# Message stage: segment sums of two groups in one pass of four column strips, gathers held once a piece

## The reference

```
xs = concat(x[src, :8], x[dst, :8]);  xv = concat(x[src, 8:], x[dst, 8:])   # 16 scalars, 16 vectors
h  = sqrt(2) * relu(emb @ W1 / sqrt(10));  w = (h @ W2 / 4).reshape(E, 7, 16, 8)
s, g  = scalar and gate sums over u of xs, (xv . y1), each times w      # 8 and 8 of an edge
v     = vector sums over u of xs * y1, xv, W3J(xv, y2), each times w    # 8 x 3 of an edge
msg   = concat(G * tanh(s), (G * tanh(g))[:, None] * v) * weight[:, None]
out   = segment_sum(msg, dst)
```

## Time and profile before

| | us |
|---|---|
| median of 3 runs | 5658.57 |
| lowest and highest | 5657.39, 5661.72 |
| profiled execution, device time | 5663.47 |
| its span | 5661.7 |
| loop of the first message stage | some 740 to 3230 |

### The profile page before, as it was taken

The page is one execution under the profiler, slowest core; times in us unless marked ns, Lnnn a source line. Parts: engine busy times, 40 slices in busy tenths (PEclk is TensorE's granted clock), DMA queues, the critical chain, the costliest instruction groups (busy, mean ns, idle before and its releaser), DMA issues. The chain is left out here.

```text
span 5661.7 us, 70210 instructions
## 1 busy us (share of the span) xinstructions
PE 4006.7 (71%) x20839; PEld 2129.7 (38%) x20839; DVE 3192.8 (56%) x5351; ACT 1475.9 (26%) x2862; POOL 3379.2 (60%) x3371
## 2 busy tenths in 40 slices
PE   0005888787888888877877860099898998999870
PEld 0002322222222222232222320077666666766650
DVE  4504776776767776677776763044444444455442
ACT  2002444444444444444444430000000000001000
POOL 5675555555555555555555417666666666666756
PEclk9999888888888888888888985599999989999985
DMA  8411111111111111111111101022222222222211
GB/s 300 114 38 18 38 37 36 37 37 37 37 35 33 36 37 31 34 37 37 37 37 37 35 18 22 18 41 45 43 43 43 42 43 43 43 42 48 46 27 24
DMA packets 266652, 252.42 MB, mean 45 GB/s; under 512 B 182208, under 2 KB 236936, under 8 KB 263777
## 3 DMA queue, kind: packets, MB, share of 16 engines
q1 hardware_dynamic: 157028, 174.83, 11.2%
q0 software_dynamic: 109024, 72.30, 9.0%
q10 hardware_dynamic: 462, 4.00, 0.2%
HBM read 160.54 MB, written 90.34 MB: 44 GB/s over the span
## 5 line engine op out<-in xcount | busy, mean ns | idle before, releaser
L612 POOL DMA_INDIRECT edge<-xp_d,idx x1440 | 1421.4, 987 | 1089.0 <-issue 419.4
L864 DVE TENSOR_TENSOR prod<-G_ps,hid 128x1000 f32<-128x1000 f32 x1200 | 1399.4, 1194 | 884.6 <-remote 410.6
L1198 POOL DMA_INDIRECT gxb<-tab_d,idxb x1200 | 1259.1, 1049 | 577.0 <-issue 334.4
L753 PE MATMUL G_ps<-FT,wst 32*128 32x500 f32 x4800 | 999.3, 685 | 362.7 <-DVE prod L864 244.4
L1233 PE MATMUL G_ps<-tb,hot 125*126 125x500 f32 (+1 forms) x3200 | 727.8, 378 | 395.5 <-DVE hotk L1255 301.1
L782 PE MATMUL R_ps<-prod,red 128*32 128x500 f32 x4800 | 923.8, 706 | 0.8 <-ACT rt L678 0.8
L1233 PEld LDWEIGHTS G_ps<-tb,hot 125*126 125x126 f32 x3200 | 572.0, 201 | 537.5 <-issue 446.8
L753 PEld LDWEIGHTS G_ps<-FT,wst 32*128 32x128 f32 x4800 | 270.7, 200 | 827.5 <-DVE prod L864 412.3
L773 PE MATMUL T_ps<-FT,wst 32*128 32x500 f32 x800 | 522.4, 737 | 3.1 <-issue 3.1
L666 ACT ACTIVATE FT<-T_ps 128x500 f32<-128x500 f32 x400 | 235.0, 588 | 856.3 <-PE G_ps L753 629.9
L782 PEld LDWEIGHTS R_ps<-prod,red 128*32 128x32 f32 x4800 | 180.8, 124 | 691.2 <-issue 445.5
(11 more groups left out here) (242 smaller groups left out, 4541.3 us busy)
## 6 DMA issues: line engine op xcount, KB each, us to landing
xd_d<-zeros SPq DMA_DIRECT2D x16, 1562.5 KB
y_d<-zrb SPq DMA_DIRECT2D x40, 595.0 KB
edge<-xp_d,idx POOLq DMA_INDIRECT x1440
xv<-xd_d SPq DMA_DIRECT2D x40, 560.0 KB
y_d<-zr SPq DMA_DIRECT2D x40, 560.0 KB
edge<-sel_d SPq DMA_DIRECT2D x40, 546.9 KB
gxb<-tab_d,idxb POOLq DMA_INDIRECT x1200
em<-in_edge_attr SPq DMA_DIRECT2D x40, 175.0 KB
```

What stands on the lines that cost most here:

```text
L612: nc.gpsimd.indirect_dma_start(out=edge_c[:, i, 8:8 + DIM], out_offset=None, in_=xp_d, in_offset=bass.IndirectOffsetOnAxis(col, 0)).then_i ...
L753: return Tn.matmul(G_ps[pair][:, a * 512:a * 512 + GW], wst[rows, r * 128:(r + 1) * 128], FT[k][rows, :], start=True, stop=True)
L864: V.tensor_tensor(prod[k][i][:, :].rearrange("p (a e) -> p a e", a=2), gv, hid[k][:, :].rearrange("p (a e) -> p a e", a=1).broadcast_to([1 ...
L1198: nc.gpsimd.indirect_dma_start(out=gx[h][:, c * T1:(c + 1) * T1], out_offset=None, in_=tab_d, in_offset=bass.IndirectOffsetOnAxis(idx[h][: ...
```

## The change

`red` gets a third block. `prod` gets four buffers a kind of product in place of two, so that both groups of a piece stand in it. The sums of a piece are made together, twelve matmuls in three rounds of four column strips (two strips a group), at three places: `sum_round` 0 behind round1 of the next even group, 1 at that group's end, 2 behind round1 of the odd group. One ScalarE copy (`rt`, 128 x 500) and four back transposes of 128 columns follow, where there were two copies and eight transposes. `Y_ps` is laid out in 64 columns an edge column. ScalarE's `high` and VectorE's `turned` and `along` run one piece further ahead, and the tail of a piece runs a group later. Waits that others cover are left out on ScalarE, VectorE and TensorE, and the semaphore `b_G` is split in `b_G` and `b_G2`. GpSimd's `pace` keeps the hold at column 0 alone, and the indices are copied eight at a time.

```
-                        if c == 2 and (not isinstance(p, int) or p > 2):
-                            hold(S("b_gs"), p * 2 - 4)
-                        if c == 5 and some(p):
-                            hold(S("b_mul"), p * 6 - 4)
...
-                                if c == 0 and s % PC == 0 and not fixed:
-                                    for q in range(s, s + PC):
-                                        hold(S(f"b_gx{q}"), t * 16 * PW + 16 * PW)
-                                    nc.gpsimd.tensor_copy(idx[:, i:i + C], src_i[:, bass.ds((p + RING) * PW, C)]).then_inc(S("b_ix"), 1)
-                                    hold(S("b_ix"), t * 2 + s // PC - 1)
+                                if c == 0 and not fixed:
+                                    nc.gpsimd.tensor_copy(idx[:, i:i + PW], src_i[:, bass.ds((p + RING) * PW, PW)]).then_inc(S("b_ix"), 1)
+                                    hold(S("b_ix"), p - RING + 1)
...
-                            if k == 1 and not (last and g + 3 >= G2):
-                                s = (g + 3) // 2
+                            if k == 0 and not (first and g < 4):
+                                tanh(t * RING + g // 2 - 2)
+                            if k == 0 and not (last and g + 4 >= G2):
+                                s = (g + 4) // 2
                                 high(t * RING + s, s % RING, t * 2 + s // PC)
+                            if k == 1 and not (first and g < 2):
+                                out_of_R(t * RING + g // 2 - 1)
...
-                        for a in range(2):
-                            for o in range(3):
-                                i = (o, (0, 2, 1)[o])[a]
-                                last = Tn.matmul(R_ps[32 * o:32 * o + 32, 0:GW], red[:, a * KF:(a + 1) * KF], prod[k][i][:, a * GW:(a + 1) * GW], start=(a == 0), stop=(a == 1))
+                    def sum_round(m, b, u):
+                        if u == 0:
+                            pe.wait_ge(S("b_mul"), m * 6 + 6)
+                            if some(m):
+                                pe.wait_ge(S("b_rt"), m)
+                        for q in range(4):
+                            pair, a = ((0, 0), (1, 0), (2, 0), (0, 1), (2, 1), (1, 1))[q % 2 * 3 + u]
+                            last = Tn.matmul(R_ps[32 * q:32 * q + 32, 0:GW], red[:, u * KF:(u + 1) * KF],
+                                             prod[b * 2 + q // 2][pair][:, a * GW:(a + 1) * GW], start=(u == 0), stop=(u == 2))
...
                             round1(n, k)
+                            if sums_due:
+                                sum_round(m, b, 2 * k)
                             if not (last and g >= G2 - 2):
                                 transposes(n + 2, g2, p2)
-                            if not (first and g < 2):
-                                back(n - 2, k)
                             round2(n, k)
                             if not (last and g == G2 - 1):
                                 hidden(n + 1, 1 - k)
-                            if not (first and g == 0):
-                                reduce(n - 1, 1 - k)
+                            if sums_due and k == 0:
+                                sum_round(m, b, 1)
+                            if sums_due and k == 1:
+                                back(m)
```

More of the change, by code:

```diff
@@ L249, in _ @@
                     nc.gpsimd.memset(edge_c[:, :, SD + 40:EW], 0.0)
-                    for i in range(2):
+                    for i in range(3):
                         blk = red[:, i * KF + i * MO:i * KF + (i + 1) * MO]
@@ L497, in gnn_resnorm_kernel @@
             hid = [sbt(f"hid{k}", [128, GW]) for k in range(2)]
-            prod = [[sbt(f"prod{k}_{i}", [128, 2 * GW]) for i in range(3)] for k in range(2)]
-            rt = [sbt(f"rt{k}", [96, GW]) for k in range(2)]
+            prod = [[sbt(f"prod{k}_{i}", [128, 2 * GW]) for i in range(3)] for k in range(4)]
+            rt = sbt("rt", [128, GW])
+            YW = 2 * KF
             O = two("O", C1 * DIM)
@@ L648, in gather_sums @@
                         act.wait_ge(S(f"b_z{h}"), t * NPC + i + 1)
-                        if some(ch):
+                        if i == 0 and some(ch):
                             act.wait_ge(S("b_st"), ch * 32)
@@ L816, in _ @@
                     turn(PAIRS - 1, last=True)
-                    reduce(NG - 1, 1)
-                    back(NG - 2, 0)
-                    back(NG - 1, 1)
+                    for u in range(3):
+                        sum_round(NPIECES - 1, 1, u)
+                    back(NPIECES - 1)
                 @block.vector
@@ L911, in turn @@
                             ch = t * 2 + h
+                            b = g % 4
                             scan = None
@@ L914, in turn @@
                                 scan = lambda: fill(gc, ch + 1, 1 - h)
-                            if 4 <= gc < 8 and not (first and h == 0):
-                                scan = lambda: sums(gc - 4, ch - 1, 1 - h)
-                            multiply(n, k, 0)
-                            multiply(n, k, 1)
-                            if k == 0 and not (first and g < 4):
-                                q = (g - 4) // 2
+                            if 5 <= gc < 9 and not (first and h == 0):
+                                scan = lambda: sums(gc - 5, ch - 1, 1 - h)
+                            multiply(n, k, b, 0)
+                            multiply(n, k, b, 1)
+                            if k == 1 and not (first and g < 5):
+                                q = (g - 5) // 2
                                 post(2, t * RING + q, q % RING // PC, q % RING % PC, t if q >= 0 else t - 1)
@@ L923, in turn @@
                                 carry_x(ch + 1, 1 - h)
-                            if gc == 3 and not (first and h == 0):
+                            if gc == 4 and not (first and h == 0):
                                 carry_sums(ch - 1, 1 - h, t - 1 + h)
-                            if k == 1 and scan:
+                            if k == 0 and scan:
                                 scan()
-                            multiply(n, k, 2)
-                            if k == 0:
-                                q = (g + 4) // 2
+                            multiply(n, k, b, 2)
+                            if k == 1:
+                                q = (g + 5) // 2
                                 more = not (last and q >= RING)
@@ L937, in turn @@
                                     along(t * RING + q, q % RING)
-                            elif not (first and g < 3):
-                                q = (g - 3) // 2
+                            elif not (first and g < 4):
+                                q = (g - 4) // 2
                                 for i in range(2):
@@ L951, in _ @@
                         fill(i, 0, 0)
-                    for p in range(2):
+                    for p in range(3):
                         turned(p, p, 0, 0, 0)
```

100 lines of the change are left out of this document (44 added, 56 removed).

## The result

| | kernel before | changed kernel |
|---|---|---|
| time, median | 5660.15 us (5657.39 to 5674.17) | 5837.16 us (5829.3 to 5850.1) |
| ratio | 1 | 1.031, 95% interval 1.028 to 1.034 |
| first message stage, us a piece | 14.66 | 15.53 |
| of it, VectorE waiting for "remote" | 2.03 | 3.09 |

What follows compares the result with a forecast made beforehand. VectorE was taken as the bound at full clock: 10.9 us a piece, plus 4.0 held and 1.0 slow, is 15.9 against 14.66. Over 200 pieces, with 4 us at the start, +252 us: 5910 us, whole range 5360 to 6450.

Steps and rivals of the forecast that it cites:

- Undisturbed piece: First message stage: two groups of 500 edges take 10.9 us where nothing disturbs, before and after the change.
- Held term: TensorE signals held during unbroken rows of eight gathers: VectorE loses 4.0 us a piece for 2.03 now, bounds 2.0 to 6.0.
- Strip sums at full clock: Loop's sums and transposes: 1.5 us less TensorE work a piece, booked as 0 because VectorE is the bound.
- Slow stretch: Half-clock time behind held signals and the loop's turn, TensorE the bound: 1.74 us a piece becomes 1.0, bounds 0 to 1.7 off.
- Waits left out and steps moved: Dropped waits and the shifted projection, HL copy and tail in the loop: 0, moved steps bounded by -0.3 and +0.3 us a piece.
- Today's holds: GpSimd's three holds in the kernel before: waits 1.6 a piece, cutting gathers into rows of four or five on average.
- Start of the stage: First message stage's start: the first hold that bites comes about one piece later, three gathers more, 4 us.
- Much slower: Rival: every row of eight gathers in the loop stays unbroken, 19.5 us a piece, +970 us, 6630 us; chance 0.12.
- No interplay: Rival: gather rows never hold TensorE, GpSimd's 11.3 us a piece is the limit, 4990 us; chance 0.07.

Runs made afterwards that it cites:

- e4: Changed kernel with the 1440 gathers of the loop's 18 turns left out, output not the reference's: 4981 us, ratio 0.880 to the kernel before.
- e9: Changed kernel with a small GpSimd clear and a hold on it ahead of columns 2, 4 and 6, rows of two gathers: 5239 us, ratio 0.935.
- e2: Kernel before with only the changed kernel's GpSimd program, one hold and eight index columns copied a piece: 5993 us, ratio 1.060.
- e5: Kernel before with the loop's 1440 gathers and the holds for their landing left out: 5023 us, ratio 0.897.
- e1: Changed kernel with the old GpSimd program put back, holds at columns 0, 2 and 5 and 40 index columns a copy: 5937 us, ratio 1.051.
- e10: Changed kernel with a small GpSimd clear and a hold on it ahead of columns 3 and 6, rows of three, three and two: 5166 us, ratio 0.922.
- e12: Kernel before, its sums and transposes kept, with the GpSimd program of e10: 5355 us, ratio 0.956.
- e3: Changed kernel with the hold of column 0, already met, repeated ahead of each of the eight gathers: ratio 1.048 to the kernel before.
- e6: Changed kernel with a small GpSimd clear, without a wait on that clear, ahead of columns 2, 4 and 6: ratio 1.037 to the kernel before.

## Why the prediction was right, and where not

- **Direction and mechanism: right.** An unbroken row of gathers holds the signals of TensorE; the changed kernel has longer rows and more held time, 3.09 against 2.03 us a piece. Taking the gathers away (e4) and spacing them (e9) both bring it to zero. That a held signal now delays the HL copy, and with it the next row, is in the trace too.
- **Undisturbed piece, 10.9 us: right.** e4 has 10.77, with VectorE busy 95%; the last turn of the changed kernel has clock 1.00.
- **Held term, 4.0 us a piece: the mis-sized term.** It measured 3.09. The sum was 0.8 x 3.5 for rows cut by a scan and 0.2 x 6.0 for whole ones. Counted over the 122 pieces from 1000 to 2900 us, 59 have no spacing above 1.5 us in their row, and lose 3.9 us each; the other 63 lose 2.3 us each. Whole rows were more common than booked (0.48 for 0.2) and both kinds cheaper: 33 of the 129 held products start ahead of their row's last gather, where the term had every signal held until 2.46 us behind it. The two errors pull apart, so that 4.0 came as near as it did partly by luck. The gather edit alone (e2) has 3.82. Over 200 pieces the step from 2.03 to 4.0 was booked as 394 us; the gather edit alone cost 6.0% of 5660 us, 340 us.
- **Strip sums at full clock, 0: wrong.** VectorE was called the bound there, which left the sums no room. Without gathers they give 0.5 us a piece (11.27 - 10.77), a third of the 1.5 us priced for the case without cover. VectorE is busy 1174 of 1300 us in e5 and 1230 in e4: the old order left it waiting for a tenth of the time, the new one for a twentieth. The 10.89 us was one good piece of the kernel before, not what its loop does undisturbed.
- **Slow stretch, 1.74 falling to 1.0 us: wrong, its size luck.** Beside the measured floors (11.27 in e5, 10.77 in e4) and the held time, 1.36 us are left in the kernel before, 1.31 in e2 and 1.67 in the changed kernel: this part did not fall. In rows of eight the sums do give 0.87 us a piece (16.40 - 15.53) where 0.74 was booked here, but as a lower floor (0.50) and shorter held time (0.73), less 0.36 that this rest grew.
- **Waits left out and steps moved, 0: not refuted in this pairing, wrong as a rule.** The HL copy comes half a piece sooner and the tail half a piece later; the prediction had one piece and a quarter of one. With the old holds this turns three holds into one, and the sum half costs 5.1% (e1). That old holds stop working when other engines' steps move was no step of the prediction. The price of the waits left out alone wasn't measured.
- **Today's holds.** They were counted as 60, 76 and 75 waits from the earlier trace rows. GpSimd waits for the HL copy ahead of the index copy too, in 22 pieces more, so it is 1.8 a piece, not 1.6; rows of four to five on average stand.
- **Start of the stage, 4 us.** No run prices it alone. The loop's first gather goes out at 602.5 us where it was 590.1; ten pieces at 0.87 us are 8.7 of these 12.4, which leaves room for the 4.
- **The sum.** 252 forecast, 177 measured. By halves: gathers 394 booked and some 340 measured, sums and transposes 148 booked as gained and some 164 measured (1.060 - 1.031 of 5660 us). Of the missing 75 us, 54 are the gathers' term and 16 the sums'. That the sums' total fits is luck, as said above: it was booked in the wrong place.
- **Rivals.** Much slower (19.5 us a piece) did not come: whole rows of eight are half of all, but no held wait of VectorE is longer than 5.2 us. No interplay is refuted as a description of this kernel. Its 4990 us stands beside the 4981 of e4 by coincidence: it was priced from GpSimd's 11.3 us a piece, and e4 has no gathers in the loop to take them. e10, with all of them, comes within 5% of e4 (0.922 against 0.880). The rule of the Trainium skill weighed there (SBUF — State Buffer, Who interferes with whom) is one on ports and doesn't cover the signals of TensorE beside a train of gathers: held 3.09 us a piece with them, 0 without.

## What to carry to other kernels

Where GpSimd issues row gathers beside TensorE work, try them in rows of two or three with a pause that GpSimd makes itself (a tiny instruction and a hold on it, 0.6 us more a row); here this turned a 3% loss into an 8% gain, and on the kernel before, with its old sums, a 4% gain (e12). Holds on other engines are no pacing to rely on: they are met or not as those engines' programs shift, so an edit elsewhere can undo them. When two edits are made together, run each alone and both: here each half alone was worse than both.

## What the hardware showed that was not expected

- A met hold, or a clear of 0.12 us, costs nothing between two gathers (1.25 us apart with and without, e3 and e6). With a hold on that clear the next gather starts 0.78 us behind the clear's end, and the spacing is 1.85 us (e9).
- A gather of 64 rows is hardly shorter than one of 125 (948 against 979 ns), and holds signals back as much.
- Without gathers in the loop the clock stands at 1.00 (e4), with rows of three at 0.94, with rows of eight at 0.83: most of the low clock comes and goes with the rows. Held signals are not its only cause: rows of two have none and stand at 0.91, with a longer piece (12.70 us) than rows of three (12.07).
- What in the chip delays the signals isn't known from these runs: only that the train of gathers does, that rows of three still hold a few (0.51 us a piece), and that a spacing of 1.85 us after every second gather leaves none.
